# First cross attention: for six of sixteen tiles, contexts with keys on the lanes made by TensorE transposes and ScalarE copies in place of a second load

## The reference, cut to what matters

```python
x = x + _L0_xattn_ref(_layernorm(x), ctx, ctx, mask, Wq, bq, Wk, bk, Wv, bv, Wo, bo, g0, beta0)
# per sequence b of 64, 32 query rows, 257 keys, 256 features, float32:
#   scores = (xn Wq + bq) (ctx[b] Wk + bk)^T / 16, masked keys get -1e9, softmax over the keys
#   out    = layernorm(((probs (ctx[b] Wv + bv)) Wo + bo)) * g0 + beta0
```

## Time and profile before

| quantity | value |
|---|---|
| median of three runs | 1634.19 us |
| the profiled execution's own time | 1632.93 us |
| its span in the trace | 1631.1 us |
| granted clock of TensorE, mean | 0.97 |
| bytes moved | 203.97 MB, mean 125 GB/s |
| PE, DVE, ACT, POOL busy over the span | 92%, 67%, 50%, 36% |
| this stage | from the start to about 142 us |

### The profile page before, as it was taken

One profiled execution on the slowest core, in us unless ns is written; L12 is line 12 of the kernel. 1 busy time (PEld: TensorE's weight loads), 2 busy tenths in 40 slices (PEclk: granted clock), 3 DMA queues, 4 the chain that ended last, 5 costly groups with the idle time before them and its releaser, 6 DMA issues. The chain is left out here.

```text
span 1631.1 us, 38596 instructions
## 1 busy us (share of the span) xinstructions
PE 1495.9 (92%) x15236; PEld 1160.9 (71%) x15236; DVE 1099.4 (67%) x2415; ACT 812.2 (50%) x1847; POOL 585.6 (36%) x487
## 2 busy tenths in 40 slices
PE   6897989899998999999999888999799688999998
PEld 4444467555576579999998746666688677799997
DVE  4687879982047555565562567888599677668787
ACT  1233742121134336666663448999277322666664
POOL 2430300000011027676654256787288452121210
PEclk9999989999999999999999999999999798999999
DMA  9991059621024367666648416664000010000001
GB/s 324 357 349 49 1 172 216 129 56 46 1 78 136 95 219 251 224 254 247 250 173 202 115 44 229 209 204 142 27 1 1 17 30 16 0 27 27 27 1 52
DMA packets 114075, 203.97 MB, mean 125 GB/s; under 512 B 38073, under 2 KB 74361, under 8 KB 108009
## 3 DMA queue, kind: packets, MB, share of 16 engines
q1 hardware_dynamic: 91481, 107.69, 22.3%
q0 software_dynamic: 10032, 57.55, 10.1%
q10 hardware_dynamic: 12384, 36.27, 6.8%
HBM read 161.63 MB, written 39.83 MB: 124 GB/s over the span
## 5 line engine op out<-in xcount | busy, mean ns | idle before, releaser
L2369 POOL TENSOR_TENSOR a_pr<-a_pr,a_inv 128x1028 f32<-128x1028 f32 x64 | 122.2, 1910 | 63.8 <-DVE a_inv L2496 63.8
L380 PE MATMUL ps<-kv_ctx,kv_w 128*128 128x257 f32 x464 | 125.1, 406 | 7.2 <-PEq L1577 2.4
L384 PE MATMUL ps<-kv_w,kv_ctx 128*128 128x256 f32 x464 | 118.0, 399 | 11.6 <-ACT kv_kv L404 11.6
L2460 ACT ACTIVATE a_pr<-ps,a_neg 128x257 f32<-128x257 f32 x256 | 119.0, 473 | 1.7 <-DVE a_neg L2512 1.7
L1613 POOL TENSOR_TENSOR b0m_pm<-b_dr,b_gates 128x256 f32<-128x256 f32 x16 | 13.2, 831 | 290.3 <-SPq L1577 261.4
L2512 DVE TENSOR_REDUCE a_neg<-ps 128x2 f32<-128x514 f32 x128 | 87.8, 688 | 39.9 <-PE ps L2386 38.9
L384 PEld LDWEIGHTS ps<-kv_w,kv_ctx 128*128 128x128 f32 x464 | 89.9, 200 | 32.9 <-ACT kv_kv L404 18.8
L380 PEld LDWEIGHTS ps<-kv_ctx,kv_w 128*128 128x128 f32 x464 | 88.0, 201 | 25.9 <-issue 10.5
L3366 DVE SCALAR_TENSOR_TENSOR x<-ps,g_gate,x 128x256 f32<-128x256 f32 x256 | 105.1, 475 | 0.0
L2397 PE MATMUL ps<-ident,a_pr 128*128 128x128 f32 x512 | 81.2, 282 | 17.0 <-ACT a_prT L2467 11.6
L964 DVE SCALAR_TENSOR_TENSOR b_F<-b_F,b_fir 128x992 f32<-128x992 f32 (+29 forms) x128 | 96.5, 790 | 0.0
(11 more groups left out here) (442 smaller groups left out, 4444.2 us busy)
## 6 DMA issues: line engine op xcount, KB each, us to landing
late_kv<-kv SPq DMA_DIRECT2D x52, 513.0 KB, 4.2
kv<-kv_kv ACTq DMA_DIRECT2D x46, 513.0 KB
a_ctxT<-in_ctxT SPq DMA_DIRECT2D x32, 514.0 KB, 8.9
a_ctxR<-in_ctx SPq DMA_DIRECT2D x32, 512.0 KB
kv_ctx<-in_ctxT ACTq DMA_DIRECT2D x34, 257.0 KB
kv_ctx<-in_ctxT SPq DMA_DIRECT2D x24, 257.0 KB
outs<-f_yo SPq DMA_DIRECT2D x16, 256.0 KB
a_vB<-vlast SPq DMA_DIRECT2D x32, 128.0 KB
```

Of the source, the lines that this page charges most:

```text
L380: done = e.matmul(out[:, 0:NK], self.w[:, 0, c, cols(part)], ctx[:, c, :], start=(c == 0), stop=(c == DC - 1))
L384: done = e.matmul(out[:, cols(t, D)], ctx[:, c, cols(t)], self.w[:, 1, c, :], start=(c == 0), stop=(c == DC - 1))
L2369: e.tensor_tensor(pr[:, b % RP, :, :], pr[:, b % RP, :, :], inv[:, b % 2, :].unsqueeze(2).to_broadcast([P, HG, NK]), ALU.mult).then_inc(*p ...
L2460: e.activation(pr[:, b % RP, r, :], K.ps[:, bank(b, r), 0:NK], ACT.Exp, bias=neg[:, b % 2, r:r + 1], accum_out=tot[:, b % 2, r:r + 1]).the ...
```

## The change

A tile t is turned if t >= 4 and t is even: 4, 6, 8, 10, 12, 14. For these `values(t)` no longer issues the two loads of `ctxR`, only the one of `ctxL`. In their place TensorE transposes the context from `ctxT`: for each half c of the keys (128 each) and for each pair of the four sequences a "fill" of four 128 x 128 transposes into one bank (6 or 7 by turns), and ACT copies each fill (128 x 512) from PSUM to `ctxR`. The c = 0 half is made in step t, the c = 1 half in step t+1; so each of the steps 4 to 15 has two fills. A fill waits until ACT has copied the fill two before it. The weighted sum of a turned tile waits for its four copies; `queries`, which uses the same banks, waits for all copies so far; `keys(t)` waits until the tile whose place it takes has been turned.

```diff
+        def is_turned(t):
+            return t >= GT and t % 2 == 0
+        def fills(t):
+            return 4 * sum(is_turned(u) for u in range(t))
+        def values_sent(t):
+            return sum(16 if is_turned(u) else 48 for u in range(t % KS, t + 1, KS))
...
                     if t >= KS:
                         e.wait_ge(*t_sc.at(t - KS + 1))
+                    if t >= KS and fills(t - KS + 1):
+                        e.wait_ge(*t_cx.at(fills(t - KS + 1)))
...
-                    for c in range(2):
+                    for c in range(0 if is_turned(t) else 2):
                         e.dma_start(ctxR[:, s, c, :, :], I["ctx"][t, :, c, :, :]).then_inc(*l_val[s].up(16))
...
+                    if fills(GT * g):
+                        e.wait_ge(*a_cx.at(fills(GT * g)))
...
+                def turn_context(t, c):
+                    for half in range(2):
+                        n = fills(t) + 2 * c + half
+                        if n >= 2:
+                            e.wait_ge(*a_cx.at(n - 1))
+                        for b in range(2):
+                            for m in range(DC):
+                                done = e.transpose(K.ps[:, 6 + half, b * D + m * P:b * D + (m + 1) * P],
+                                                   ctxT[:, t % KS, 2 * half + b, m, cols(c)], K.ident[:, :])
+                        done.then_inc(*t_cx.up())
...
                 def weigh(t):
-                    e.wait_ge(*l_val[k].at(48 * (t // KS + 1)))
+                    e.wait_ge(*l_val[k].at(values_sent(t)))
+                    if is_turned(t):
+                        e.wait_ge(*a_cx.at(fills(t + 1)))
...
                     if tile(t - 1):
                         turn_probs(t - 1)
+                    for c in range(2):
+                        if tile(t - c) and is_turned(t - c):
+                            turn_context(t - c, c)
                     if tile(t - 2):
                         weigh(t - 2)
...
+                def context_turned(t, c):
+                    for half in range(2):
+                        e.wait_ge(*t_cx.at(fills(t) + 2 * c + half + 1))
+                        if t >= KS:
+                            e.wait_ge(*t_pv.at(t - KS + 1))
+                        e.activation(ctxR[:, t % KS, c, 2 * half:2 * half + 2, :],
+                                     K.ps[:, 6 + half, :].rearrange("p (b d) -> p b d", b=2), ACT.Copy).then_inc(*a_cx.up())
...
                     if tile(t):
                         exponents(t)
+                    for c in range(2):
+                        if tile(t - c) and is_turned(t - c):
+                            context_turned(t - c, c)
                     if tile(t - 2):
                         mixed(t - 2)
```

More of the change, by code:

```diff
@@ L542, in cross_attention_0 @@
         t_w, t_x, t_kq, t_sc, t_prT, t_pv, t_mixT, t_o = Y.sigs_of("pe", "w x kq sc prT pv mixT o")
+        t_cx, a_cx = Y.sig("pe", "ctxturned"), Y.sig("act", "ctxtaken")
         mask_rows = I["mask"].rearrange("b q k -> b (q k)")
```

## The result

The changed kernel took 1645.35 us, the median of nine runs (1637.89 to 1651.81), beside 1634.16 us for nine runs of the kernel before (1625.51 to 1640.04): ratio 1.0071, 95% interval 1.0042 to 1.0101. It is slower by 11 us, 7 to 16 with the interval. Single executions of either kernel spread over 15 us and more, so the time says that the change is slower, and the timeline says where.

A forecast was written before the change was run, and what follows sets the result against it. The prediction took TensorE to bound the stage from step 4 on, not the loads. Transposes adding 11.52 us, less 2.56 hidden, gave +9.0 us: 1643.2 us predicted, with 1637.5 to 1649 as the 8-in-10 range.

The forecast's parts named there:

- step 7 to the queries: Loop step 7: without DVE's mask wait, 6.57 us to the queries against 6.16 before; 0.55 us of the transposes hidden.
- step 11 to the queries: Loop step 11: two ACT copies stand before the queries; 6.95 us against 6.21, 0.74 added, 0.22 hidden.
- step 15 and up to DVE's addition for tile 12: Loop's end and first weighted sum: exponent wait goes, tile 14's copies cost some 0.4 us; 0.68 of 0.96 hidden.
- TensorE sets the pace: From step 4 on TensorE, at 4.84 us a step, limits the stage; DVE is level in steps 8 to 15.
- A transpose costs 0.12 us: Steps 4 to 15: eight transposes each, 0.12 us apiece, 0.96 us a step, 11.5 us in all.
- ACT's copies are hidden but for the queries of step 11: 24 copies at 0.598 us, 14.4 us on ACT, fit its idle time; exceptions counted in the step terms.
- The loads that go are worth the waits of steps 6 and 7: Twelve loads removed save only 0.18 us in step 6 and DVE's 1.01 us mask wait for tile 7.
- Rival 1: Loads set the pace: 17 to 18 us go, transposes fill part; about -6 us, 1628; chance 0.06.
- Rival 2: Transposes cost 0.159 us each, or TensorE waits for ACT each step: +12.8 us, up to 1 more, 1647; chance 0.22.
- rival 3: More is hidden: transposes at 0.09 us, DVE's level steps 8 to 15 hide 4 us; +4.5, 1638.7; chance 0.14.
- Rival 4: Transposes lower TensorE's clock to 1.2 GHz in the twelve loop steps: +70 us, 1700; chance 0.01.
- The stage's end at 151 us, later stages as before: First stage ends at about 151 us instead of 142; all later stages as long as before.

The follow-up runs named there:

- e1: Kernel before without the two ctxR loads of tiles 4, 6, 8, 10, 12, 14, nothing in their place; ratio to before 0.9999.
- e2: Kernel before with all loads kept plus the 96 transposes on TensorE, no ACT copies, result unused; ratio to before 1.0062.
- e3: The change with all loads kept, ACT copying the transposed contexts into a spare tile nobody reads; ratio to before 1.0112.
- e5: Kernel before with values of tiles 1 and 2 loaded after keys and masks of tiles 2 and 3; ratio to before 1.0017.
- e9: Kernel before, unchanged, run again for a second trace; ratio 1.0026, 90.34 us from step 4's start to the stage's end.
- e4: The changed kernel, run again unaltered; ratio to before 1.0045, 99.87 us from step 4's start to the stage's end.
- e8: The change plus values of tiles 1 and 2 loaded after keys and masks of tiles 2 and 3; ratio to before 1.0049.
- e6: The changed kernel's code with tile 2 alone turned, all others loaded; no ratio, 90.75 us from step 4's start to the stage's end.
- e10: The kernel with tile 2 alone turned (e6), run again; ratio to before 1.0064, 90.64 us from step 4's start to the stage's end.

## Why the prediction was right, point by point

The direction and the mechanism held, and the size nearly: forecast +9.0 us, measured +11.2 in the medians and +7.95 to +9.5 in the stretch that the change touches. 1645.35 lies within the stated 1637.5 to 1649, 2 us above the 1643.2. The terms, by start-to-start distances of the first trace against the earlier trace rows:

| term | forecast | measured |
|---|---|---|
| steps 4, 5, 8, 12, 14, each | +0.96 | +0.87, 0.88, 0.87, 0.89, 0.87 |
| step 6 | +0.78 | +0.70 |
| step 7 to the queries | +0.41 | +0.19 |
| steps 9 and 10 | +1.59 | +1.42 |
| step 11 to the queries | +0.74 | +0.53 |
| step 13 | +0.36 | +0.15 |
| step 15 and up to DVE's addition for tile 12 | +0.28 | +0.57 |
| sum | +8.96 | +7.94 |

- *TensorE sets the pace.* Shown by e1 and e2: without the loads the stretch is as long as before with a dip (90.53 and 90.34), and the transposes alone add 9.0 us to that.
- *A transpose costs 0.12 us.* It costs 0.11 in a row of eight (0.96 us from the first to what follows, less the 0.08 that a change of kind took before). This is the one size that was off in most steps, by 0.08 us a step, 1 us in all. Beyond it, the terms of steps 7, 11 and 13 came out some 0.13 us lower each and the last one some 0.37 us higher, which nearly cancels.
- *ACT's copies are hidden but for the queries of step 11.* Two copies take 1.05 us and not 1.15, and step 11 gained 0.53. At the end the prediction had the wrong semaphore: it counted 0.4 us of waiting for tile 14's copies, but the mix of tile 13 stands behind these copies in ACT's order (134.23), and the weighted sum waits for it to be out of its bank, 0.81 us. The prediction had named the mix as queued behind the copies and had not followed it to this place.
- *The loads that go are worth the waits of steps 6 and 7.* The waits went, as forecast, but not because of the loads. e3 keeps all loads, has no dip, and takes 5.71 us for step 6 and 10.95 for step 7, as the change does (5.72 and 10.94). What hides these waits is TensorE's longer step. The sum is the same, since the prediction counted them once, as hidden time.
- *Rival 1* is refuted by e1: the transfers fell from a share of 1.03 to 0.87 (60 to 80 us) and the time stayed. *Rival 2* by the 0.11 and by idle time of zero at the fills; *rival 3* by the sum. *Rival 4* by the clock of 1.00 from 60 to 140 us in e2 and in all three traces of the change. The dip of 38 to 55 us lies before the first transpose and shows without any in e1, e5 and e9.
- *The stage's end at 151 us, later stages as before.* The end was at 154.59 in the first trace, with 5.0 us of that from before step 4, and at 151.29 and 151.68 in e4 and e8. The later stages took 1482 to 1485 us in the three traces of the change and 1489 to 1490 in the two of before.

What is not settled is the difference between 8 to 9.5 us in the stage and 11.2 in the medians. The interval (7 to 16 us) holds both, and e4's (0 to 15) too. The later stages, shorter in the change's traces, don't account for it. With intervals of this width it is in part luck that the median came within 2 us of the forecast; what supports the forecast is the stretch.

## What to carry to other kernels

A full transfer path is no bound by itself: look whether the engine that sets the steps has idle time that a transfer ends, and if it has none, moving bytes onto that engine costs their full instruction time, here 0.88 us for each eight transposes, and gives back at most the few waits that the trace names. The same exchange is worth trying only in the steps in which that engine stands idle for data (here steps 0 to 3, one tile: about 0.7 us, within what traces differ by). When whole times spread by 15 us, a stretch between two fixed instructions spreads far less, and an effect of 8 us stands out in one trace of each kernel. But three equal traces of one kernel (99.84, 99.87, 99.91) don't make every kernel reproducible: the two of the other differ by 1.55 us. An effect of 1 us needs several traces of both kernels, or a comparison step by step.

## What the runs showed that I had not expected

The granted clock in the first 55 us differs between executions of one kernel: 1.00 in one trace of the kernel before, 0.80 in another; 0.60 and 0.81 in the change. In the eight traces with a dip TensorE's longest wait for keys or for DVE between 30 and 48 us had been 1.41 (e2) to 3.28 us (e1); in the four without it was 0.61 (e6, e10), 1.10 (before) and 1.20 us (e3). The two groups don't overlap, but the gap between 1.20 and 1.41 is small, and no run set the wait by itself: that the wait causes the dip was not shown. Another order fits nearly as well: step 0 had started at 29.5 or later in three of the four traces without a dip, and at 28.3 or earlier in all eight with one; only e6 (27.84, no dip) breaks it. Where step 0 starts early (27.56 in e9 instead of 29.54), the wait is the longer, since tile 3's keys don't land earlier; a faster start is then lost again. The 18 us by which the mixture of experts varied (e1, e6, e10) go with a fall of the same kind at 875 to 925 us.
